# Weighing in halves from step 0, the first rows of maxima ahead of stack 3, and the last turn of maxima behind a weighing

## The reference

```python
# z is the layer's input, seen as (8, 256, 256); the kernel computes 4 sequences
zn  = (z - mean(z)) / sqrt(var(z) + 1e-05) * ln_w + ln_b
qkv = zn @ W_qkv + b_qkv            # 16 heads of 16 channels
scores = einsum('bhqd,bhkd->bhqk', q, k) / sqrt(16)
attn = softmax(scores, axis=-1)
msa  = einsum('bhqk,bhkd->bhqd', attn, v)
out  = z + msa @ W_proj + b_proj
```

## Time and profile before

| | |
|---|---|
| median of 3 runs (lowest to highest) | 1815.46 us (1814.65 to 1816.88) |
| the profiled execution's own time | 1812.12 us |
| its span, from first to last instruction | 1810.6 us |
| mean granted TensorE clock | 0.948 |
| TensorE busy | 1628.5 us, 90% |
| VectorE busy | 1276.1 us, 70% |
| ScalarE busy | 838.1 us, 46% |

### The profile page before, as it was taken

One profiled execution on the slowest core, in us unless ns is written; L12 is line 12 of the kernel. 1 busy time (PEld: TensorE's weight loads), 2 busy tenths in 40 slices (PEclk: granted clock), 3 DMA queues, 4 the chain that ended last, 5 costly groups with the idle time before them and its releaser, 6 DMA issues.

```text
span 1810.6 us, 30829 instructions
## 1 busy us (share of the span) xinstructions
PE 1628.5 (90%) x10370; PEld 972.4 (54%) x10370; DVE 1276.1 (70%) x2551; ACT 838.1 (46%) x1255; POOL 251.3 (14%) x255
## 2 busy tenths in 40 slices
PE   5978999996699998889999978989997989999895
PEld 2757888885343336655433556543345654333564
DVE  3672322211589996968999688789978868997686
ACT  1302233331337784242677624257772343778412
POOL 0143222222200120200003030100203010000020
PEclk8988999998789999998999989999998998999998
DMA  3128877774312310004222000412300031220000
GB/s 130 50 71 218 271 220 235 227 228 146 61 31 37 72 37 1 1 6 90 34 40 72 2 1 1 93 21 37 76 15 1 1 65 33 37 34 2 1 1 24
DMA packets 80205, 123.39 MB, mean 68 GB/s; under 512 B 13529, under 2 KB 55770, under 8 KB 80042
## 3 DMA queue, kind: packets, MB, share of 16 engines
q1 hardware_dynamic: 70666, 93.46, 20.1%
q0 software_dynamic: 9376, 27.80, 5.3%
HBM read 76.84 MB, written 18.61 MB: 53 GB/s over the span
## 4 chain that ended last, share of the span: by engine, by line
PE 68%; DVE 16%; issue 6%; ACT 4%; SPq 3%; POOL 1%; DMA 1%; DVEq 0%; ACTq 0%; POOLq 0%
PE PS L1030 13%; PE PS L987 10%; PE PS L901 8%; PE PS L913 7%; PE PS L1145 6%; DVE MX L1517 6%; PE PS L1017 5%; PE PS L1155 5%; SPq L439 3%; PE PS L960 2%; PE PS L852 2%; PE PS L1104 1%; ACT Pb L720 1%; PE PS L1175 1%; PE PS L891 1%
## 5 line engine op out<-in xcount | busy, mean ns | idle before, releaser
L1517 DVE TENSOR_REDUCE MX<-PS 128x1 f32<-128x512 f32 x1024 | 635.7, 683 | 44.3 <-PE PS L987 41.8
L720 ACT ACTIVATE Pb<-PS 128x1024 f32<-128x1024 f32 x512 | 511.1, 1026 | 176.9 <-PE PS L1017 176.6
L987 PE MATMUL PS<-Ks,Qs 48*128 48x512 f32 x1024 | 395.8, 469 | 9.5 <-DVE MX L1517 5.4
L1017 PE MATMUL PS<-Qs,Ks 50*128 50x512 f32 x1024 | 336.0, 462 | 18.2 <-ACT Pb L720 11.6
L1030 PE MATMUL PS<-Pb,V 128*32 128x256 f32 x4096 | 315.5, 398 | 1.0
L987 PEld LDWEIGHTS PS<-Ks,Qs 48*128 48x128 f32 x1024 | 163.1, 189 | 225.7 <-DVE MX L1517 203.2
L1030 PEld LDWEIGHTS PS<-Pb,V 128*32 128x32 f32 x4096 | 91.6, 110 | 161.8 <-ACT Pb L720 84.9
L1413 DVE TENSOR_TENSOR V<-PS,V 128x512 f32<-128x512 f32 x39 | 27.0, 691 | 203.9 <-PE PS L913 203.9
L1017 PEld LDWEIGHTS PS<-Qs,Ks 50*128 50x128 f32 x1024 | 134.8, 190 | 54.4 <-ACT Pb L720 37.9
L913 PE MATMUL PS<-Pb,OT 128*128 128x256 f32 x624 | 141.0, 379 | 0.0
L643 ACT ACTIVATE OT<-PS,b1t 128x256 f32<-128x256 f32 x156 | 65.5, 471 | 158.8 <-PE PS L901 158.8
(11 more groups left out here) (286 smaller groups left out, 1897.9 us busy)
## 6 DMA issues: line engine op xcount, KB each, us to landing
Pb<-W SPq DMA_DIRECT2D x78, 512.0 KB, 4.0
y_slot<-V SPq DMA_DIRECT2D x39, 256.0 KB, 3.8
Qs<-Qh SPq DMA_DIRECT2D x128, 64.0 KB, 2.3
Ks<-Kh SPq DMA_DIRECT2D x120, 64.0 KB, 2.4
V<-b SPq DMA_DIRECT2D x39, 128.0 KB, 3.6
XT<-x_mid POOLq DMA_DIRECT2D x4, 1024.0 KB, 6.5
out<-Pb POOLq DMA_DIRECT2D x4, 1024.0 KB, 6.9
OT<-xT SPq DMA_DIRECT2D x2, 1024.0 KB, 6.3
```

The source lines that it names most:

```text
L720: F["ex"].inc(act.activation(Pb[:, kt % 2, 2 * qh:2 * qh + 2, :], PS[:, 2 * qh:2 * qh + 2, :], ACT.Exp, scale=0.25))
L987: F["slp"].inc(pe.matmul(PS[:, slot_bank(i), :], Qs[rows, p % NB, t * P:(t + 1) * P], Ks[rows, p % NB, kh * HALF:(kh + 1) * HALF], start=T ...
L1017: ins = pe.matmul(PS[:, 2 * qh + a, :], Ks[rows, p % NB, kt * P:(kt + 1) * P], Qs[rows, p % NB, qh * HALF:(qh + 1) * HALF], start=True, st ...
L1517: F["sld"].inc(dve.tensor_reduce(MX[:, p % 2, a, t, kh:kh + 1], PS[:, slot_bank(i), :], AX.X, ALU.max))
```

## The change

Three edits.

1. `FIRST` is 0 instead of 12: steps 0 to 11 use the order in halves too. In step 0 there is nothing yet to weigh, hence `if apart and m`.
2. SP issues the rows of maxima of pair 0 after the stacks of pairs 0 to 2 and ahead of the stack of pair 3.
3. `turn_max(7)` moves from the middle of step 53 to its end, behind both halves of `weigh(52)`.

```diff
-                for p in range(NB):
+                for p in range(NB - 1):
                     stack(p)
                 maxima_row(0)
+                stack(NB - 1)
                 for p in range(NB, NP):
                     maxima_row(p - NB + 1)
                     stack(p)
...
-                FIRST = 12
+                FIRST = 0
                 LAST = (NP * UN - UN - LEAD) // 4
...
                         transposed_scores(p, kt, qh)
-                        if qh and m == LAST:
-                            turn_max(NP - 1)
                         maxima(ahead + (2 if not qh else step if apart else 3))
-                        if apart:
+                        if apart and m:
                             weigh(m - 1, qh)
                     if not apart:
                         for qh in range(2 if m else 0):
                             weigh(m - 1, qh)
                         maxima(ahead + step)
+                        if m == LAST:
+                            turn_max(NP - 1)
```

## The result

The changed kernel is slower. Its median is 1832.82 us in 5 runs (1820.32 to 1842.53), against 1816.29 for the kernel before in 5 runs on the same chip (1814.65 to 1819.31). The ratio is 1.0083, its 95% interval 1.0051 to 1.0116. Ratios in this text leave out executions more than 1.5% above the fastest of their kernel, so they need not be the quotient of the two medians.

What follows compares the result with a forecast made beforehand. TensorE and VectorE bound steps in halves; in steps 0 to 11 VectorE idles some 8 us a sequence. Savings of 9.5 + 1.2 = 10.7 us off the median 1815.46 gave 1805 us, range 1788 to 1824.

Steps and rivals of the forecast that it cites:

- 38.0 us from the copy to step 12 with the clock up: Each sequence, VectorE's copy of pair 0's rows to step 12: 38.0 us at full clock, against 44.05 to 44.68 before.
- 0.37 us per microsecond at the half level: Steps in halves win nothing at half level, so each microsecond there takes 0.37 us off the full-clock saving.
- If the stretches stay as they are: Early steps: half-level stretches remain 44.3 us in total, costing 16.4 of 25.9 us and leaving 9.5.
- The rival with the other sign: Steps 1 to 11 and later: half level lasts longer without whole weighings, slower, 1823 or 1841 us; chance 0.26.
- break-even of 73 us in total: Half-level stretches of 73 us over four sequences, 18.3 each, would cancel the gain of 27.1 us.
- The argument that outweighed it: Early steps: fuller work around the half-level stretch speaks against longer stretches; no size given.
- The argument against: Early steps: the level rose in all four cases behind a whole weighing, which the new order lacks; suggests longer stretches.
- Where the first half weighing comes: First sequence, step 1: the first half weighing starts at about 518.5, where the level fell (518.60).
- VectorE never lacking a unit: Steps 0 to 11 in halves: VectorE lacks a unit no longer than a half weighing, 0.57 us at full level.
- Edit 2: Rows ahead of stack 3: 3.6 us earlier in all, already in the sum; alone in the old order 0 to 3.6.
- Edit 3: Step 53, last turn behind the weighing: next scores 0.3 us earlier per sequence, 1.2 us in all; cover 0.7 us.
- the first rival: Early steps: the clock doesn't fall, or only in one sequence; 27.1 us saved, time 1788 us; chance 0.19.

Runs made afterwards that it cites:

- fill_light: The changed kernel plus three small unread matmuls, two ahead of the wait for rows, one in step 0: 1861.64 us, ratio 0.9949 to the kernel before.
- halves_only: The kernel before with only the order in halves from step 0: 1889.18 us, ratio 1.0172.
- rows_only: The kernel before with only the rows of maxima issued ahead of stack 3, whole order kept: 1858.9 us, ratio 1.0008.
- turn_only: The kernel before with only the last turn moved behind the weighing in step 53: 1860.41 us, ratio 1.0003.
- one_piece: The changed kernel with both half weighings of steps 1 to 5 together behind scores 1: 1845.32 us, ratio 0.9888 to the kernel before.
- first_six_whole: The changed kernel with steps 0 to 5 kept in the whole order (FIRST = 6): 1854.08 us, ratio 0.997 to the kernel before.
- all_three: The changed kernel unaltered, run on the third chip beside the kernel before: 1879.04 us, ratio 1.0028.
- one_piece_all: The changed kernel with the weighing in one piece in all steps up to 52, no filling: 1873.5 us, ratio 1.0029 to the kernel before.
- halves_filled: The changed kernel plus seven small unread matmuls in steps 0 and 1: 1838.59 us, ratio 0.9896 to the kernel before.

## Why the prediction was wrong, by its own steps

**38.0 us from the copy to step 12 with the clock up: right.** fill_light measured 38.03 and 37.98 (with three small matmuls, two of them in a wait; its step 0 takes 2.48 us, as in the changed kernel). That it agrees to the tenth is luck: from the copy to the first exponential it took 3.67 us instead of 3.35, and the rest took 34.36 instead of 34.7. In the changed kernel itself the case never occurred.

**0.37 us per microsecond at the half level: right.** The four rows of the table give 0.34 to 0.37. The step behind it was put at 4.8 us; its exponentials in the trace lie 4.75 us apart. PE's timeline of the changed kernel shows one half step at the half level, and then the first units behind the rise at 547.27. Records overlap, so starts are compared:

```profile
540.83 0.79 PE L988 MATMUL PS<-Ks,Qs 48*128 48x512 f32 x1
540.83 1.22 PE L1018 MATMUL PS<-Qs,Ks 50*128 50x512 f32 x2
...
541.98 1.08 PE L1031 MATMUL PS<-Pb,V 128*32 128x256 f32 x8
542.99 0.79 PE L988 MATMUL PS<-Ks,Qs 48*128 48x512 f32 x1
...
547.31 0.50 PE L988 MATMUL PS<-Ks,Qs 48*128 48x512 f32 x1
...
548.54 0.50 PE L988 MATMUL PS<-Ks,Qs 48*128 48x512 f32 x1
```

From unit to unit it takes 542.99 - 540.83 = 2.16 us at the half level and 548.54 - 547.31 = 1.23 at the full one, where the earlier trace rows had 1.24.

**"If the stretches stay as they are, 13.65 + 10.23 + 6.81 + 13.65 = 44.3 us in total": this is the step that failed.** They became 116.1 us in the profiled execution, 2.6 times as long. By the prediction's own formula, 25.9 + 1.2 - 0.37 x 116.1 = -15.9: a loss of 16 us. The execution that has these 116.1 us lost 8.2 in its span: the half level cost 40.0 us instead of 43.0, steps 12 to 20 gave 2.1 that the prediction had put at nothing ("the change does nothing here"), and the stages ahead happened to take 2.9 less. That the median, 1832.8, lies close to 1815.5 + 15.9 = 1831 is therefore no test of the formula. The median execution wasn't profiled; by its mean clock it had (1 - 0.922) x 2 x 1831.3 = 286 us of half level over the whole span, some 27 more than the profiled one. The rival with the other sign was right in its mechanism, longer stretches, and the time falls between its two cases, 1823 and 1841; its break-even of 73 us in total was passed, at 27 to 31 us a sequence against the 18.3 it needed. The argument that outweighed it, that the work around the stretch is fuller, carried nothing: TensorE was busy for all of the 116 us. The argument against, that the level had risen four times out of four behind a weighing in one piece and that the new order has none, pointed the right way. It deserved more than 0.26.

That the division itself makes the stretches longer is shown by halves_only against rows_only and turn_only (191 us of half level against 58 and 48), and by one_piece (51 us, with 10.24 in place of 27 to 31 for a first stretch). Counted over all traces without filling, the first stretch of a sequence lasted 23.9 to 58.0 us in all 12 that began in halves, and 6.8 to 17.1 us in 22 of the 24 that began with weighings in one piece. The other two are those of first_six_whole, so one piece makes an early rise likely and doesn't force it. That the clock, and not the order, costs the time is shown inside fill_light.

**Where the first half weighing comes.** It was put at 518.5, "right where the level fell". All starts 2.9 us earlier here, so read it against the first scores: in the first sequence these come at 512.6, and the half weighing 3.5 us behind them (predicted 3.1). The level falls at 516.55, while it runs. PE's timeline of the changed kernel:

```profile
512.62 0.49 PE L988 MATMUL PS<-Ks,Qs 48*128 48x512 f32 x1 [0.71 <-DMA Qs<-MR]
...
516.12 0.71 PE L1031 MATMUL PS<-Pb,V 128*32 128x256 f32 x8
```

It did not hold the level. So the fall in this sequence comes 3.9 us behind the scores (3.2 before), hardly moved; it is the rise that moved.

**VectorE never lacking a unit: right at the full level only.** Its idle time of 1.68 us is gone; at the half level it waits for TensorE behind two or three units each time. VectorE's timeline of the changed kernel:

```profile
522.33 1.89 DVE L1518 TENSOR_REDUCE MX<-PS 128x1 f32<-128x512 f32 x3 [0.87 <-PE PS L988]
524.92 1.29 DVE L1518 TENSOR_REDUCE MX<-PS 128x1 f32<-128x512 f32 x2 [0.70 <-PE PS L988]
```

In fill_light's first sequence it runs 20 units on end:

```profile
518.37 12.04 DVE L1526 TENSOR_REDUCE MX<-PS 128x1 f32<-128x512 f32 x20
```

**Edit 2: right.** SP's row DMAs go out 0.1 us behind the copy, where they were up to 2.43 us late. SP's timeline, sequences 1 to 3, with the end of stack 3 in the first:

```profile
509.82 1.39 SPq L448 DMA_DIRECT2D Qs<-MR  x2
511.25 0.56 SPq L439 DMA_DIRECT2D Qs<-Qh  x1
...
518.19 0.59 SPq L439 DMA_DIRECT2D Ks<-OT  x1
...
844.96 1.36 SPq L448 DMA_DIRECT2D Qs<-MR  x2
...
1178.90 1.35 SPq L448 DMA_DIRECT2D Qs<-MR  x2
```

Stack 3 is out by 518.8 and delays nothing that the trace shows. In the old order the edit is worth nothing that can be seen, as read from the earlier trace rows.

**Edit 3: right.** PE's timeline of step 53, which answers to the earlier trace rows:

```profile
666.76 1.11 PE L1018 MATMUL PS<-Qs,Ks 50*128 50x512 f32 x4
667.80 1.07 PE L1031 MATMUL PS<-Pb,V 128*32 128x256 f32 x16
668.80 0.28 PE L995 MATMUL PS<-ident,NMs 128*32 128x128 f32 x1
669.01 0.77 PE L1018 MATMUL PS<-Qs,Ks 50*128 50x512 f32 x4
```

The turn has no wait, and the next scores follow 2.25 us behind the first instead of 2.57. The step from first exponential to first exponential takes 2.27 us where it took 2.57: 0.3 us in each sequence, 1.2 in all. Step 56, which uses the rows, takes 2.8 us as before, so the cover of 0.7 us was enough.

**The rule from the Trainium skill.** The Trainium skill (TensorE: Matmul & The Clock Gate, section HAM oscillation) ties the fall of the level to waits of TensorE for DMAs. From it the prediction concluded, beside the first rival, that shorter waits would leave the level high. The trace does not bear that out: the waits were shortened in sequences 2 and 3, and the level fell in all four, behind a wait of 0.71 to 0.73 us. As a cause of the fall the waits are thus not excluded, but they are not what sets the length: in 116 us TensorE waited for nothing.

**Left open.** What exactly lifts the level. It rose behind whole weighings in one_piece, but it also rose in the middle of halves, after 24 to 58 us, without one, and in first_six_whole five whole weighings didn't lift it. Whether the small matmuls hold the level by their work or by what they shift in time: a pause of the same length was not tried. And why the kernels in halves had 191 us on one chip and 130 on another, with edits 2 and 3: those are two single executions, and stretches differ by 20 us within one. The gain of one_piece in its runs (0.0112 x 1864.46 = 20.9 us, at least 11 by the interval) is more than its early windows explain (4.4 us, 2.1 in steps 12 to 20, 1.2 for the turn). Where the rest lies isn't shown: the kernel before was not profiled on that chip. Against all_three on the same chip the early windows, 24.0 us shorter, more than cover the 19.8 us between the two spans.

## What to carry to other kernels

A reordering that wins at TensorE's full level can lose by keeping the engine at half level. Cost it at both levels, and don't carry the length of the low one over from the old trace: look there for what TensorE was doing each time the level rose, and ask whether the new order still does it. That is a warning sign and not a rule, as first_six_whole shows. Work in one piece at the start, or a few full-array matmuls that nobody reads (seven with the halves, four with the whole order), were each worth about 1% here; three and five with the halves about half of that. Halves paid from then on: one_piece_all, which never splits the weighing, lost the gain again.

## What the runs showed of the hardware that was not expected

- TensorE with at most 0.1 us of gap in its records stayed at 1.2 GHz for 23.89 to 58.03 us, with half weighings between units and scores of 48 and 50 rows. The same matmuls with the weighing in one piece had the level back after 10.24 us in all eight sequences of one_piece and one_piece_all. Yet in first_six_whole it stayed low for 25.64 us with five weighings in one piece among them.
- With the halves, three small matmuls kept the level from falling at the start in 2 of 4 sequences, five in 2 of 4, seven in 4 of 4. Between the two outcomes a window differs by 9.2 us in one execution.
- Stretches at half level differ between executions of one kernel, and with them its run times: 22 us of spread instead of 5 on the first chip. On the third it is 35 us in 12 runs, where the kernel before spreads over 29 in 28, and 8 us in 12 with the weighing in one piece throughout.
- On the second and third chip every profiled kernel lost time from about step 37 of sequences 1 to 3 on, and none in sequence 4. In these steps GpSimd gathers for the next sequence (halves_filled, from 957.99 us on); the fourth has no next. In halves_filled TensorE waits for VectorE, which itself had waited for TensorE just before, and the level falls there for 27.3 us from 976.92. PE's timeline of halves_filled:

```profile
976.57 0.52 PE L988 MATMUL PS<-Ks,Qs 48*128 48x512 f32 x1 [1.19 <-DVE MX L1529]
```

And VectorE's:

```profile
975.83 2.48 DVE L1529 TENSOR_REDUCE MX<-PS 128x1 f32<-128x512 f32 x4 [1.50 <-PE PS L988]
```

The first chip has these gathers in the same steps too (in the kernel before from 624.42 us on) and none of the waits. So what starts the waits stays open.
